# Fetching the last tile of 22 edge groups row by row on SyncE instead of by a GpSimd gather

## The reference

```python
q = (xp @ Wq[l] + bq[l]).reshape(n, H, HD)      # H = 8 heads of HD = 16
k = (xp @ Wk[l] + bk[l]).reshape(n, H, HD)
v = (xp @ Wv[l] + bv[l]).reshape(n, H, HD)
att = jnp.einsum('ehd,ehd->eh', q[dst], k[src]) / scale
att = nan_to_num(clip(att, -50, 50))
ex = jnp.exp(att - m[dst]);  s = segment_sum(ex, dst)
msg = (v[src] * alpha[:, :, None]).reshape(-1, D)     # alpha = ex / s[dst]
aggr = segment_sum(msg, dst)
x = x + (aggr @ Wo[l] + bo[l])
x = x + gelu(layernorm(x) @ W1[l] + b1[l]) @ W2[l] + b2[l]
```

## Time and profile before

| | |
|---|---|
| median of three runs | 2799.0 us |
| span of the profiled execution (first to last instruction) | 2183.8 us |
| difference of the two | 615.2 us |
| DVE busy | 1710.2 us, 78% |
| POOL busy | 1570.6 us, 72% |
| PE busy | 1419.8 us, 65% |
| ACT busy | 940.2 us, 43% |
| DMA engines, mean busy share: gathers' queue, SP's queue | 33.8%, 10.3% |

### The profile page before, as it was taken

How to read it: one execution, slowest core, us unless ns; L and a number is a source line. 1 busy time by engine, 2 the same in 40 slices (tenths; PEclk the granted TensorE clock), 3 DMA queues, 4 the chain that set the end, 5 groups by cost and what they waited for, 6 DMA issues and landing times.

```text
span 2183.8 us, 32409 instructions
## 1 busy us (share of the span) xinstructions
PE 1419.8 (65%) x8227; PEld 1237.3 (57%) x8227; DVE 1710.2 (78%) x5103; ACT 940.2 (43%) x2179; POOL 1570.6 (72%) x1669
## 2 busy tenths in 40 slices
PE   4866576666667676766666657566666757666666
PEld 4555565656555565655556556556555656555555
DVE  8759888888877878787877777777777778777775
ACT  8334353534535353534454335343343435343344
POOL 6277777777777777777727777777777777777773
PEclk9979888877878788887988787787787778787787
DMA  2365445444444444444424444444444444444441
GB/s 87 119 178 182 148 133 154 147 136 134 142 134 125 142 134 142 124 142 134 132 69 143 135 125 136 137 123 139 133 139 124 139 134 129 134 134 138 125 138 56
DMA packets 123505, 289.29 MB, mean 132 GB/s; under 512 B 31525, under 2 KB 57057, under 8 KB 123329
## 3 DMA queue, kind: packets, MB, share of 16 engines
q0 software_dynamic: 77824, 212.31, 33.8%
q1 hardware_dynamic: 45504, 74.92, 10.3%
HBM read 275.44 MB, written 8.38 MB: 130 GB/s over the span
## 4 chain that ended last, share of the span: by engine, by line
POOL 47%; issue 20%; DVE 11%; PE 11%; DMA 6%; ACT 3%; DVEq 1%; SPq 0%; ACTq 0%
POOL kvr L801 47%; DMA kvr<-kv_table,srcidx 5%; PE bank L1079 4%; PE bank L1092 3%; DVE agg L1706 3%; DVE kvr L1322 2%; DVE prod L1675 1%; DVE msg L1697 1%; ACT apart L1279 1%; ACT onehotT L1283 1%; DVE onehot L1667 1%; PE bank L1036 1%; PE bank L1015 1%; PE bank L816 1%; PE bank L894 1%
## 5 line engine op out<-in xcount | busy, mean ns | idle before, releaser
L801 POOL DMA_INDIRECT kvr<-kv_table,srcidx x1612 | 1530.7, 950 | 547.4 <-issue 480.0
L1079 PE MATMUL bank<-q,onehotT 128*128 x3320 | 606.8, 340 | 712.1 <-DVE prod L1675 475.2
L1079 PEld LDWEIGHTS bank<-q,onehotT 128*128 128x128 f32 x3320 | 515.6, 237 | 825.5 <-issue 824.8
L1092 PE MATMUL bank<-msg,onehot 128*128 128x136 f32 x3320 | 612.3, 344 | 1.9 <-DVE msg L1697 1.9
L1289 ACT ACTIVATE bank<-attc 128x32 f32<-128x32 f32 x404 | 81.2, 201 | 1145.7 <-DVE attc L1691 1145.0
L1092 PEld LDWEIGHTS bank<-msg,onehot 128*128 128x128 f32 x3320 | 571.8, 252 | 3.6 <-DVE msg L1697 3.3
L1675 DVE TENSOR_TENSOR prod<-kvr,bank 128x512 f32<-128x512 f32 x404 | 276.0, 683 | 302.6 <-DMA kvr<-kv_table,srcidx 264.0
L1706 DVE TENSOR_TENSOR agg<-agg,bank 128x136 f32 x1624 | 469.1, 289 | 44.9 <-PE bank L1092 40.1
L1279 ACT ACTIVATE apart<-relT,minus_p 128x512 bf16<-128x512 bf16 x416 | 293.8, 706 | 4.4 <-DMA relT<-rel_table 4.0
L1667 DVE TENSOR_TENSOR onehot<-bank,rel 128x512 f32<-128x512 f32 x416 | 282.5, 682 | 0.2
L1697 DVE TENSOR_TENSOR msg<-kvr,bank 128x512 f32<-128x512 f32 x404 | 273.9, 678 | 5.0 <-ACT bank L1289 4.9
(11 more groups left out here) (217 smaller groups left out, 844.5 us busy)
## 6 DMA issues: line engine op xcount, KB each, us to landing
relT<-rel_table SPq DMA_DIRECT2D x104, 512.0 KB, 4.1
kvr<-kv_table,srcidx POOLq DMA_INDIRECT x1612
loop_kv<-kv_table SPq DMA_DIRECT2D x25, 128.0 KB, 3.9
kv_table<-qkv SPq DMA_DIRECT2D x25, 128.0 KB, 3.2
kv_table<-onehot SPq DMA_DIRECT2D x8, 256.0 KB, 2.2
w<-weights SPq DMA_DIRECT2D x2, 840.0 KB, 7.4
loops<-x_in SPq DMA_DIRECT2D x5, 320.0 KB, 5.6
q<-qkv SPq DMA_DIRECT2D x25, 64.0 KB
```

The costliest lines, as they stand in the source:

```text
L801: pool.indirect_dma_start(kvr[:, n % RING, j, :], None, kv_table[l], bass.IndirectOffsetOnAxis(ap=srcidx[:, step:step + 1], axis=0)).then_ ...
L1079: mm = pe.matmul(bank[2][:, j * D:(j + 1) * D], onehotT[:, m % OHT, j, :], q[:, bass.ds(ranks[j + h], 1), :].rearrange("p a c -> p (a c)") ...
L1092: mm = pe.matmul(sum_ps(n, k), onehot[:, m % OH, j, :], msg[:, n % 2, j, :], start=(m, j) == of[0], stop=(m, j) == of[-1])
```

## The change

Of each layer, the groups 31, 47, ..., 191 (eleven, every sixteenth) are rowed: GpSimd issues three gathers for them instead of four. Their fourth tile is fetched by SyncE into a buffer of its own, `rowkv` (two of them), with one DMA a row: 128 DMAs a tile, each with the node's number in a register. They stand in the sixteen slots g-22 to g-7, eight rows a slot, with one register load of eight numbers ahead of them. The numbers come from `srcrow`, which SyncE fills with eleven small DMAs at the beginning, once the tables of source nodes have arrived. VectorE's product and message of a rowed group are done in two instructions each: one for three tiles and one for the fourth.

```diff
+ROWED = tuple(range(31, 192, 16))
+ROWS_A_SLOT, ROWS_LEAD, ROW_BUFS = 8, 6, 2
+ROW_SLOTS = P // ROWS_A_SLOT
+ROW_LOAD = 8
...
+def pooled(n):
+
+    return gathers(n) - is_rowed(n)
...
+            sp.wait_ge(s_rows, 16 * 2 * SC)
+            for i, g in enumerate(ROWED):
+                chunk, step = divmod(row_of(g, at_begin=True) + G - 1, P)
+                sp.dma_start(srcrow[0:1, i * P:(i + 1) * P], step_src[step:step + 1, chunk * P:(chunk + 1) * P]).then_inc(s_srcrow, 16)
...
+            def fetch_tile_rows(l, g, part):
+
+                n = l * GROUPS + g
+                i = rowed_no(n)
+                if part == 0:
+                    if i >= ROW_BUFS:
+                        before = (i - ROW_BUFS) // len(ROWED) * GROUPS + ROWED[(i - ROW_BUFS) % len(ROWED)]
+                        sp.wait_ge(s_msg, before + 1)
+                    if l == 0:
+                        sp.wait_ge(s_first_table, 16 * len(KV_PAIRS))
+                    else:
+                        for u in range(2):
+                            c = NCH - 1 - u
+                            sp.wait_ge(s_table[buffer(l, c)], stored(l, c))
+                for p0 in range(part * ROWS_A_SLOT, (part + 1) * ROWS_A_SLOT, ROW_LOAD):
+                    at = ROWED.index(g) * P + p0
+                    nodes = nc.values_load_multi_w_load_instructions(srcrow[0:1, at:at + ROW_LOAD], engines=(ENG.SP,), min_val=0, max_val=NP - 1,
+                                                                     skip_runtime_bounds_check_because="the number of a node")[1]
+                    for j, node in enumerate(nodes):
+                        sp.dma_start(rowkv[p0 + j:p0 + j + 1, i % ROW_BUFS, :, 0:D], kv_table[l][bass.ds(node, 1), :].rearrange("a (h c) -> a h c", h=2)).then_inc(s_rowkv[i % ROW_BUFS], 16)
...
                     if (l, s) == (0, 2 * BODY):
                         load_x0()
+                    for g in ROWED:
+                        if 0 <= s - (g - ROWS_LEAD - ROW_SLOTS) < ROW_SLOTS:
+                            fetch_tile_rows(l, g, s - (g - ROWS_LEAD - ROW_SLOTS))
...
-                for j in range(gathers(n)):
+                for j in range(pooled(n)):
...
-                t = gathers(n)
-                dve.tensor_tensor(prod[:, 0:t, :], kvr[:, n % RING, 0:t, 0:D], bank[2][:, 0:t * D].rearrange("p (j c) -> p j c", c=D), ALU.mult).then_inc(s_prod, 1)
+                t = pooled(n)
+                ins = dve.tensor_tensor(prod[:, 0:t, :], kvr[:, n % RING, 0:t, 0:D], bank[2][:, 0:t * D].rearrange("p (j c) -> p j c", c=D), ALU.mult)
+                if is_rowed(n):
+                    i = rowed_no(n)
+                    dve.wait_ge(s_rowkv[i % ROW_BUFS], 16 * P * (i // ROW_BUFS + 1))
+                    ins = dve.tensor_tensor(prod[:, t, :], rowkv[:, i % ROW_BUFS, 0, 0:D], bank[2][:, t * D:(t + 1) * D], ALU.mult)
+                ins.then_inc(s_prod, 1)
```

More of the change, by code:

```diff
@@ L168, in is_seam, with is_rowed, rowed_no @@
     return n % GROUPS < SEAM_GROUPS
+def is_rowed(n):
+    return n % GROUPS in ROWED
+def rowed_no(n):
+    return n // GROUPS * len(ROWED) + ROWED.index(n % GROUPS)
+def pooled(n):
+    return gathers(n) - is_rowed(n)
 def row_of(n, at_begin=False):
@@ L201, in landed @@
 def landed(n):
-    return 16 * sum(gathers(k) for k in range(n % RING, n + 1, RING))
+    return 16 * sum(pooled(k) for k in range(n % RING, n + 1, RING))
 def blocks_by(c):
@@ L329, in build @@
         kvr = sb("kvr", [P, RING, G, KV])
+        rowkv = sb("rowkv", [P, ROW_BUFS, 2, D])
+        srcrow = sb("srcrow", [1, len(ROWED) * P], I32)
         onehot = sb("onehot", [P, OH, G, P])
@@ L504, in build @@
         s_kv = [sem(f"s_kv{r}") for r in range(RING)]
+        s_srcrow = sem("s_srcrow")
+        s_rowkv = [sem(f"s_rowkv{u}") for u in range(ROW_BUFS)]
         s_oh = sem("s_oh")
@@ L649, in _ @@
                 sp.dma_start(table[:, b0:b0 + nb, :], kv_of(b0, nb)).then_inc(s_first_table, 16)
+            sp.wait_ge(s_srcrow, 16 * len(ROWED))
             for c, (b0, nb) in enumerate(NAT):
@@ L1695, in edge_msg @@
                 dve.wait_ge(s_ex, n + 1)
-                t = gathers(n)
-                dve.tensor_tensor(by_head(msg[:, n % 2, 0:t, 0:D]), by_head(kvr[:, n % RING, 0:t, D:KV]),
-                                  ex[:, 0:t * H].rearrange("p (j h) -> p j h", h=H).unsqueeze(3).broadcast_to([P, t, H, HD]), ALU.mult).then_inc(s_msg, 1)
+                t = pooled(n)
+                ins = dve.tensor_tensor(by_head(msg[:, n % 2, 0:t, 0:D]), by_head(kvr[:, n % RING, 0:t, D:KV]),
+                                        ex[:, 0:t * H].rearrange("p (j h) -> p j h", h=H).unsqueeze(3).broadcast_to([P, t, H, HD]), ALU.mult)
+                if is_rowed(n):
+                    ins = dve.tensor_tensor(msg[:, n % 2, t, 0:D].rearrange("p (h d) -> p h d", d=HD), rowkv[:, rowed_no(n) % ROW_BUFS, 1, 0:D].rearrange("p (h d) -> p h d", d=HD),
+                                            ex[:, t * H:(t + 1) * H].unsqueeze(2).broadcast_to([P, H, HD]), ALU.mult)
+                ins.then_inc(s_msg, 1)
             def edge_add(n, j, ranks):
```

## The result

The changed kernel takes 3030.4 us (median of 4 runs, 3027.4 to 3041.0), the kernel before 2798.1 beside it: a ratio of 1.0847, 95% interval 1.0822 to 1.0873. I had forecast 2804, with 2900 as the upper end. It is 232 us slower, in the direction of rival B.

A forecast was written before the change was run, and what follows sets the result against it. POOL's gathers were taken as the bound. SP's late relT load adds 18.7 us in the first layer, fewer gathers save 13.8 in the second: +4.9 on 2183.8, plus 615.2 around the span, gives 2804 us; own range 2785 to 2830, eight-in-ten 2769 to 2900.

The forecast's parts named there:

- rival B: SP sets the pace in both layers at `fetch_tile_rows`, from 4.82 us a slot on; 2906 or 3194 us; chance 0.23.
- Around the span lie 615.2 us, which I take as unchanged: Time outside the profiled span of 2183.8 us, by the median of the runs, added to the forecast.
- POOL sets the pace: POOL issues gathers 1.2525 us apart, 806 filling 1010 us of each layer, waiting on DVE only 11.2 us.
- the gain by 22 fewer: On POOL, 22 gathers of 1.2525 us left out save 27.6 us, 13.8 a layer.
- A slot of rows is 4.77 us: SP's time for eight rows of 0.525 us and one register load of 0.57, against POOL's mean slot of 4.93.
- the load of eight: SP's register load of eight node numbers, taken as two fours: 0.50 us, 0.57 with gaps.
- My bounds, 4.41 to 5.92: SP's slot in us: rows at 0.505 and load 0.37, up to rows at 0.525 and load 1.72.
- B's formula: Total shift of both layers in us, 351 s - 1683, s being SP's slot of rows, beyond s = 4.82.
- the copies: SP's three copies into one partition, 0.717 us each, a reason for a dearer row of 0.90.
- The deadline: SP's relT load for group 190, due by 1050.3 us; about 15 us late before ACT waits; rows have none earlier.
- DVE's split instructions: DVE's product and message in two parts: 0.3 us a rowed group, 6.6 in all, hidden by gather waits, charged 0.
- the sign that I had named for B: In the profile after, ACT waits for relT in the second layer too, not in the first alone.

The follow-up runs named there:

- e11: The kernel before with only the gathers of the first eight groups, later groups computing on stale rows: 2012.0 us, ratio 0.7120.
- e2: The changed kernel without SyncE's rows, 22 gathers left out, DVE's split instructions kept (wrong result): 2745.9 us, ratio 0.9812.
- e10: The changed kernel with all rows on SyncE, but only the gathers of the first eight groups: 2043.6 us, ratio 0.7237.
- the second trace: The kernel before, profiled again without any edit: 2793.6 us, span 2791.9.
- e5: The changed kernel with the bodies' relT loads issued by ACT instead of SyncE: 3037.2 us, ratio 1.0844.
- e3: The changed kernel with every row DMA at a constant address, no register loads or steps (wrong rows): 2796.5 us, ratio 0.9990.
- e15: The changed kernel with each GpSimd gather replaced by a plain load of 128 neighbouring rows, SyncE's rows kept: ratio 0.7215.
- e14: The kernel before with each gather replaced by a plain load of 128 neighbouring rows by GpSimd: ratio 0.7082.
- e6: The changed kernel with five rowed tiles a layer instead of eleven, four rows a slot instead of eight: 2813.5 us, ratio 1.0041.
- e4: The changed kernel with seven rows of eight at constant addresses, loads of eight kept (wrong rows): 2798.0 us, ratio 0.9984.
- e13: The kernel before with all gathers, each fetching 128 B of a row instead of 1 KB from the ring's fourth turn on: ratio 0.9968.

## Why the prediction was wrong, step by step

**"Around the span lie 615.2 us, which I take as unchanged": this step failed first.** In every timed run beside the experiments 1.7 to 2.0 us lie there. A span so far from the run's time was the sign that the profiled execution was another kind than the timed ones, and I wrote it down without asking what it meant for the rows. In that execution DVE had no such gaps at its sums, 40.1 us of waits for PE in all. In the timed ones it has 618.7 us of them. That this is near the 615.2 may be a coincidence; no run here tells. For the execution of the first trace the reading was right, POOL set its pace: it took 2183.8 us where the kernel without gathers takes 2012.

**"POOL sets the pace": wrong for the timed executions.** POOL waits 607.3 us for DVE where the earlier trace rows had 11.2. Without any gathers before it, DVE, PE and ACT need 2012 us (e11), 813 less, so in the timed executions the gathers cost time by something other than POOL's 1.25 us a piece. Hence the gain by 22 fewer was also mis-sized: 54 us (e2) and not 27.6.

**"A slot of rows is 4.77 us": the term that made the sign.** Its parts: a row was priced 0.525 and takes 0.41 undisturbed (15.45 us for 32 rows and the three loads between them in e10, less 3 x 0.78); the load of eight was priced 0.50 and takes 0.72 to 0.78. Undisturbed a slot is 4.2 with its share of `relT` (e10), better than I had reckoned. In the changed kernel it is 7.2: the steps beside the gathers are longer than anything in the rows that I priced from. My bounds, 4.41 to 5.92, were all drawn from steps of 37 to 43 and 332 to 355 ns; the same line of the second trace of before shows what they miss:

```profile
L672 SPq FUSED_REGOPS  x25: 3/37/714, 256.5 to 622.3; - x25
L672 SPq DMA_DIRECT2D loop_kv<-kv_table x25: 3/332/1385, 256.7 to 623.0; - x25
```

**Rival B's mechanism was right, its size was not, and its reasons only in a small part.** SP sets the pace in both layers, and ACT waits for `relT` (399.6 us). B's formula says 351 s - 1683, which for 7.2 would be +844, since it started from a pace of 4.93 us a slot; the true pace of before is 6.54, and SP exceeds it by some 0.65. That is why a slot that is dearer by half than reckoned costs only 8%. By the prediction's own terms the second layer begins to lose at s = 4.84 and not at 4.82, a slip that changes nothing here. Of B's reasons, the copies don't hold: a row's DMA has a median of 0.228 us and not 0.717. The load of eight is dearer than two fours, as B had it, but takes 0.72 to 0.78 us and not the 1.65 of one value after the other. What B lacked is that the steps themselves grow longer beside the gathers. The Trainium skill, Runtime: NRT & Kernel Launch (section on instruction fetch mechanics), has about 200 ns for each register, which would be 1.6 us, an estimate; the trace disagrees, 0.716. The page describes this load as one from device memory, while `srcrow` lies on the chip.

**The deadline was well placed.** `relT` is the first to suffer. But it isn't the only one: with `relT` out of the way (e5), the rows' own product waits instead, 207.9 us, at the same total.

**Small steps that held.** DVE's split instructions cost 6.8 us of busy time (1717.0 against 1710.2) where 6.6 was reckoned, and e2, which has them, is faster than before. POOL has 1590 gathers, still 0.30 us of issue apart. ACT waits for `relT` in both layers (186.6 and 213.0 us), the sign that I had named for B.

**What stays open.** The cause of the long steps and of the gaps at DVE's sums, and why the first profiled execution had neither. And the 51 us by which e3 (constant addresses) stands above e2: SP has 1082 us to spare there and ACT doesn't wait for `relT`, so it isn't the budget. In e10 and e15, beside no gathers, the rows cost 32 and 37 us, and there most of it is the budget again: ACT waits 24.8 and 36.2 us for `relT`, against 4.8 (e11) and 3.4 (e14). No version that fetches the right rows (the changed kernel and e6) beats the kernel before; e3 and e4, with wrong rows, are within 0.2% of it.

## What to carry to other kernels

Compare the span of the profiled execution with the time of the runs before reading a row of it; where they are 600 us apart, the profile is of something else, and one more profile costs little. Work moved to an idle queue is cheap only up to a budget, the others' pace (here it cost some 50 us even inside it), and its price must be read from how long that queue takes over a whole stretch while the rest of the kernel runs, not from its median step. And an operation's price may lie with others: take it out once and see what the kernel loses, before moving a twentieth of it elsewhere.

## What the runs showed that I had not expected

- With GpSimd's 1612 indirect DMAs the timed kernel takes 41% longer than with plain loads of the same bytes (2799 us against 1983, e14), with POOL busy for only 56% in the one and 45% in the other, and waiting for DVE in both. Cutting the queue's bytes from 212 to 38 MB changes 0.3% (e13). The first trace, 2183.8 us with the same 1612, shows that they don't always cost this.
- Beside indirect DMAs single steps of SyncE's sequencer last up to 1.4 us instead of 0.03 (register steps) and 0.23 (DMA issue), 603 of 5632 register steps over 0.4 us; beside plain loads none of 5632 is over 47 ns (e15). VectorE's register steps stay at 65 ns or less in both.
- TensorE's mean granted clock, as a share of full speed, differs too: 0.68 with the gathers, 0.81 in the first trace and 0.87 with plain loads (e14), though PE does the same matmuls. It isn't shown whether the higher clock is a cause or an effect of the shorter kernel.
- One kilobyte in one row costs SyncE 228 ns to issue by the median, against 320 for `relT` and 342 for blocks of 128 partitions; a register load of eight values 716 (after) to 779 ns (e10).
